# Feed-forward weight slices in four buffers, loaded in one schedule across the phases

## What is computed

```python
def _reference_tuple_inner(x, W_r, W_k, W_v, mu_r, mu_k):
    x_prev = jnp.concatenate([jnp.zeros((B, 1, C), x.dtype), x[:, :-1, :]], axis=1)
    xr = mu_r * x + (1.0 - mu_r) * x_prev
    xk = mu_k * x + (1.0 - mu_k) * x_prev
    r = jax.nn.sigmoid(jnp.einsum('btc,dc->btd', xr, W_r))
    k = jnp.einsum('btc,dc->btd', xk, W_k)
    k_act = jnp.square(jax.nn.relu(k))
    out = r * jnp.einsum('btc,dc->btd', k_act, W_v)
...
xn = _layernorm(x, axis=-1)
x = x + _L0_attn_ref(xn, Wq, bq, Wk, bk, Wv, bv) + _L0_ffn_ref(xn, W_r, W_k, W_v, mu_r, mu_k)
```

## Time and profile before

| | us |
|---|---|
| median of 2 runs | 5767.32 (5766.93 to 5767.71) |
| the profiled execution | 5756.6 |
| its span (slowest core, core 0) | 5755.0 |
| spans of the 8 cores | 5732.4 to 5755.0 |
| granted TensorE clock, mean of a core | 0.761 to 0.768 |
| feed-forward stage, first slice load to the last store | 866 to 2152 |
| stage of the attention | from about 2260 |

### The profile page before, as it was taken

How to read it: one execution, slowest core, us unless ns; L and a number is a source line. 1 busy time by engine, 2 the same in 40 slices (tenths; PEclk the granted TensorE clock), 3 DMA queues, 4 the chain that set the end, 5 groups by cost and what they waited for, 6 DMA issues and landing times.

```text
span 5755.0 us, 57304 instructions; the slowest of 8 cores (5732.4 to 5755.0 us)
## 1 busy us (share of the span) xinstructions
PE 3132.9 (54%) x11513; PEld 1102.6 (19%) x11513; DVE 2488.8 (43%) x5263; ACT 1707.0 (30%) x2627; POOL 286.9 (5%) x301
## 2 busy tenths in 40 slices
PE   1121203332433432777777777777777678678676
PEld 0021101111111111122222222122122123122122
DVE  3431313444343331652753753643643653653653
ACT  2300000000000000255355355355255245245255
POOL 0000010000000000000000000000000000000000
PEclk9965557677767776688788688688688689689688
DMA  1244002111211121110110110110110100100100
GB/s 61 61 78 92 5 3 52 40 40 38 51 40 48 46 57 26 28 28 11 27 28 11 27 28 12 27 28 10 28 28 5 34 19 14 34 19 14 28 19 17
DMA packets 516779, 181.70 MB, mean 32 GB/s; under 512 B 494282, under 2 KB 495474, under 8 KB 516274
## 3 DMA queue, kind: packets, MB, share of 16 engines
q1 hardware_dynamic: 482386, 130.46, 10.0%
q0 software_dynamic: 34080, 47.56, 4.5%
HBM read 142.23 MB, written 39.34 MB: 32 GB/s over the span
## 4 chain that ended last, share of the span: by engine, by line
PE 35%; DVE 21%; DMA 17%; ACT 13%; issue 10%; DVEq 1%; ACTq 1%; POOL 0%; SPq 0%; POOLq 0%
PE pS L847 9%; DVE bm L773 8%; ACT aT L862 7%; PE pO L815 7%; PE pA L762 7%; PE pA L1008 4%; PE pA L516 3%; DMA fW<-wT_r 3%; DMA fW<-wT_k 3%; PE pA L1069 2%; ACT stage L943 2%; DMA fW<-wT_v 2%; DMA nb<-norm_all 2%; DVE fA L501 2%; DVE bis_ge L409 1%
## 5 line engine op out<-in xcount | busy, mean ns | idle before, releaser
L773 DVE TENSOR_REDUCE bm<-pA 128x16 f32<-128x512 f32 x1664 | 1151.1, 692 | 605.1 <-PE pA L762 470.3
L862 ACT ACTIVATE aT<-pS 128x1024 bf16<-128x1024 f32 x1024 | 1047.7, 1023 | 772.4 <-PE pS L847 731.1
L815 PE MATMUL pO<-aT,vtm 128*65 128x512 bf16 x2048 | 698.2, 426 | 311.7 <-ACT aT L862 310.9
L762 PE MATMUL pA<-ktp,qtp 64*128 64x512 bf16 x1664 | 685.0, 422 | 312.2 <-ACT aT L862 110.3
L847 PE MATMUL pS<-rhsc,lhsc 128*128 128x512 bf16 x2048 | 714.5, 438 | 0.0
L516 PE MATMUL pA<-fA,fW 128*128 128x512 bf16 x1536 | 416.4, 424 | 282.6 <-DMA fW<-wT_r 77.4
L417 PE MATMUL pB<-bis_cnt,ones 128*128 128x32 f32 x116 | 35.2, 397 | 682.4 <-DVE bis_cnt L413 682.4
L815 PEld LDWEIGHTS pO<-aT,vtm 128*65 128x65 bf16 x2048 | 234.3, 122 | 648.5 <-issue 501.5
L773 DVE TENSOR_REDUCE bm<-pO 128x16 f32<-128x512 f32 x384 | 265.6, 692 | 212.4 <-PE pO L762 177.7
L762 PEld LDWEIGHTS pA<-ktp,qtp 64*128 64x128 bf16 x1664 | 152.4, 95 | 881.6 <-issue 878.2
L516 PEld LDWEIGHTS pA<-fA,fW 128*128 128x128 bf16 x1536 | 152.1, 106 | 541.5 <-issue 431.9
(11 more groups left out here) (150 smaller groups left out, 2542.9 us busy)
## 6 DMA issues: line engine op xcount, KB each, us to landing
xtile<-x SPq DMA_DIRECT2D x64, 512.0 KB
fW<-wT_r SPq DMA_DIRECT2D x64, 256.0 KB
fW<-wT_k SPq DMA_DIRECT2D x64, 256.0 KB
fW<-wT_v SPq DMA_DIRECT2D x64, 256.0 KB
out<-stage SPq DMA_DIRECT2D x32, 512.0 KB
rhsc<-qtp POOLq DMA_DIRECT2D x32, 256.0 KB, 3.6
lhsc<-ktp POOLq DMA_DIRECT2D x32, 256.0 KB, 2.8
bx<-bsm_dram POOLq DMA_DIRECT2D x32, 256.0 KB, 8.1
```

The source lines that it names most:

```text
L762: e.matmul(pap, qtp[p0:p0 + 64, ts0 + t * 128:ts0 + (t + 1) * 128], ktp[p0:p0 + 64, ts0 + kq * 512:ts0 + (kq + 1) * 512], start=True, stop ...
L773: e.tensor_reduce(bmp[:, kq * 16:(kq + 1) * 16], pap.rearrange("p (k e) -> p k e", e=32), axis=AX.X, op=ALU.max))
L815: e.matmul(pO[0:65, sl * 512:(sl + 1) * 512], vtm[:, (sq * 16 + k) * 130 + hip * 65: (sq * 16 + k) * 130 + hip * 65 + 65], aT[bpar][:, sl ...
L862: e.activation(aT[bpar][:, :], pS[bpar][:, :], AF.Exp, scale=0.125))
```

## The change

There are four buffers `fW` in place of two, and the 192 slice loads (8 quarters, 3 weights, 8 slices) form one list. Loads 0 to 3 are issued ahead of the loop. After the matmuls of slice i, wherever in the three phases it stands, the load of slice i + 4 is issued; it waits for the matmuls of slice i, whose buffer it takes. The last four slices of a phase so issue the first four loads of the next phase, the ones of v2 those of the next quarter. SP's wait for TensorE's counter at each phase's head is gone. The number of loads, their size, their queue and the recorder's wait between them are the same. The diff:

```diff
@@ -474,8 +474,8 @@
             fB = st_p0.enter_context(nc.sbuf_tensor("fB", [128, 8 * QT], BF))
             fR = st_p0.enter_context(nc.sbuf_tensor("fR", [128, 8 * QT], BF))
             fF = st_p0.enter_context(nc.sbuf_tensor("fF", [128, 8 * QT], BF))
-            fW = [st_p0.enter_context(nc.sbuf_tensor("fW0", [128, 8 * 128], BF)),
-                  st_p0.enter_context(nc.sbuf_tensor("fW1", [128, 8 * 128], BF))]
+            fW = [st_p0.enter_context(nc.sbuf_tensor(f"fW{j}", [128, 8 * 128], BF))
+                  for j in range(4)]
             ptile = st_p0.enter_context(nc.sbuf_tensor("ptile", [128, C], BF))
             ptileb = st_p0.enter_context(nc.sbuf_tensor("ptileb", [128, C], BF))
             ptile2 = [ptile, ptileb]
@@ -519,6 +519,21 @@
                                     start=(cc == 0), stop=(cc == 7)))
                 return r.cnt["sPE"]
 
+            wsched = [(tag, d) for _Q in range(8)
+                      for tag in ("r", "k2", "v2") for d in range(8)]
+            wst = {"ld": {}, "mm": {}}
+
+            def wload(i):
+                if i >= len(wsched):
+                    return
+                if i - 4 >= 0:
+                    r.wait("sync", "sPE", wst["mm"][i - 4])
+                tag, d = wsched[i]
+                wst["ld"][i] = load_wslice(fW[i % 4], tag, d)
+
+            for i in range(4):
+                wload(i)
+
             for Q in range(8):
                 t0 = Q * QT
                 mu_mix(fA, "r", t0)
@@ -529,20 +544,16 @@
                         emit_bisect_iter(it)
                 cons = [r.cnt["sAC"], r.cnt["sAC"]]
                 r.wait("tensor", "sDV", r.cnt["sDV"])
-                npe_hist = [0] * 8
-                r.wait("sync", "sPE", r.cnt["sPE"])
-                lds = [load_wslice(fW[0], "r", 0), load_wslice(fW[1], "r", 1)]
                 for d in range(8):
                     par = d % 2
-                    r.wait("tensor", "sSY", lds[d])
+                    gi = Q * 24 + d
+                    r.wait("tensor", "sSY", wst["ld"][gi])
                     if d == 0:
                         r.wait("tensor", "sDV", ndv_mixr)
                     r.wait("tensor", "sAC", cons[par])
-                    npe_q = mm_quarter("r", fA, d, fW[par], par)
-                    npe_hist[d] = npe_q
-                    if d + 2 < 8:
-                        r.wait("sync", "sPE", npe_hist[d])
-                        lds.append(load_wslice(fW[par], "r", d + 2))
+                    npe_q = mm_quarter("r", fA, d, fW[gi % 4], par)
+                    wst["mm"][gi] = npe_q
+                    wload(gi + 4)
                     r.wait("scalar", "sPE", npe_q)
                     cons[par] = r.emit("scalar", lambda e, d=d, par=par: e.activation(
                         fR[:, d * QT:(d + 1) * QT], pA[:, par * 512:par * 512 + QT],
@@ -556,20 +567,16 @@
                         emit_bisect_iter(it)
                 consd = [r.cnt["sDV"], r.cnt["sDV"]]
                 r.wait("tensor", "sAC", r.cnt["sAC"])
-                npe_hist = [0] * 8
-                r.wait("sync", "sPE", r.cnt["sPE"])
-                lds = [load_wslice(fW[0], "k2", 0), load_wslice(fW[1], "k2", 1)]
                 for d in range(8):
                     par = d % 2
-                    r.wait("tensor", "sSY", lds[d])
+                    gi = Q * 24 + 8 + d
+                    r.wait("tensor", "sSY", wst["ld"][gi])
                     if d == 0:
                         r.wait("tensor", "sDV", ndv_mixk)
                     r.wait("tensor", "sDV", consd[par])
-                    npe_q = mm_quarter("k2", fA, d, fW[par], par)
-                    npe_hist[d] = npe_q
-                    if d + 2 < 8:
-                        r.wait("sync", "sPE", npe_hist[d])
-                        lds.append(load_wslice(fW[par], "k2", d + 2))
+                    npe_q = mm_quarter("k2", fA, d, fW[gi % 4], par)
+                    wst["mm"][gi] = npe_q
+                    wload(gi + 4)
                     r.wait("vector", "sPE", npe_q)
                     consd[par] = r.emit("vector", lambda e, d=d, par=par: e.tensor_scalar(
                         fB[:, d * QT:(d + 1) * QT], pA[:, par * 512:par * 512 + QT],
@@ -584,18 +591,14 @@
                 r.wait("tensor", "sAC", nac_sq)
                 consd = [r.cnt["sDV"], r.cnt["sDV"]]
                 r.wait("tensor", "sAC", r.cnt["sAC"])
-                npe_hist = [0] * 8
-                r.wait("sync", "sPE", r.cnt["sPE"])
-                lds = [load_wslice(fW[0], "v2", 0), load_wslice(fW[1], "v2", 1)]
                 for d in range(8):
                     par = d % 2
-                    r.wait("tensor", "sSY", lds[d])
+                    gi = Q * 24 + 16 + d
+                    r.wait("tensor", "sSY", wst["ld"][gi])
                     r.wait("tensor", "sDV", consd[par])
-                    npe_q = mm_quarter("v2", fA, d, fW[par], par)
-                    npe_hist[d] = npe_q
-                    if d + 2 < 8:
-                        r.wait("sync", "sPE", npe_hist[d])
-                        lds.append(load_wslice(fW[par], "v2", d + 2))
+                    npe_q = mm_quarter("v2", fA, d, fW[gi % 4], par)
+                    wst["mm"][gi] = npe_q
+                    wload(gi + 4)
                     r.wait("vector", "sPE", npe_q)
                     consd[par] = r.emit("vector", lambda e, d=d, par=par: e.tensor_tensor(
                         fF[:, d * QT:(d + 1) * QT], pA[:, par * 512:par * 512 + QT],
```

## The result

The changed kernel takes 5609.6 us (median of 10 runs, 5602.9 to 5683.1) against 5766.9 (median of 8). In the run of 5683.1 us the cores of one die had a granted clock of 0.74 against 0.76 on the others, and it is left out of the ratio. The ratio, of the means of the runs, is 0.9738, with a 95% interval of 0.972 to 0.9755: 2.6% faster, about 151 us (the two medians lie 157 us apart).

The account below looks back on a forecast made before the run. Serial slice loads on SP, not TensorE, were taken to bound the feed-forward phases. Terms of 149 + 12 - 2 - 8 = 151 us took the median of 5767.3 us to a forecast of 5616 us, range 5598 to 5650.

Parts of the forecast that it names:

- What bounds a phase: In the feed-forward phases SP's loads run strictly one after the other and set the rate, about 3.04 us each.
- Part 1: Inside the 24 feed-forward phases, two of six load steps of 3.1 us fall away: 149 us gained.
- TensorE would not become the bound: In a phase, loads let slice 7 start at 16.1 us, TensorE at worst 16.0; rival chance 0.06.
- four or five slices without a gap and three behind gaps: On TensorE's trace of a phase: the first four or five slices run gapless, three gaps for loads remain.
- Part 2: At the heads of 15 r and k2 phases, the first slice starts 0.8 us sooner: 12 us gained.
- starts about 0.15 us after that: At r and k2 heads, the first slice follows the end of DVE's last bisection instruction by about 0.15 us.
- Part 3: From k2 to v2, the four early loads land with 0.5 us to spare; 2 us lost, between 0 and 11.
- Part 4: At quarter ends, the next quarter's early loads meet the stores to part_sc: 8 us lost, between 0 and 24.
- The sign of being wrong: At quarter ends, stores to part_sc taking over 3.5 us each would show the forecast wrong.
- Sum: Over the whole run, 149 + 12 - 2 - 8 = 151 us gained, to 5616 us, 2.6% less.
- The slower one: Rival: TensorE's clock stays at 1.2 GHz through whole phases, 80 us slower, 5847 us; chance 0.03.
- The one with faster loads: Rival: loads get faster and TensorE alone paces phases of about 16.2 us, gain 196 us, 5571 us; chance 0.03.

Follow-up runs that it names:

- e3: The changed kernel with eight buffers fW in place of four: 5578.8 us, 0.9691 of the kernel before.
- e4: The changed kernel, four buffers kept, with loads counted by two semaphores in turn so that two are in flight: 5556.7 us, 0.9644 of the kernel before.
- run 67: No label, but words of "made the run 67 us faster": the changed kernel with waits already covered in the same queue left out, 5542.5 us, 0.9621 of before.

## Why the prediction was right, and where its terms were off

The time was 5609.6 against 5616 predicted. By its steps:

- **What bounds a phase.** Right. The load chain is serial before and after, and the number of its steps inside a phase, not the number of buffers as such, makes the time. The kernels with two, three, four and eight buffers have phases of 23.89, 20.91, 17.84 and 16.26 us.
- **Part 1, two steps a phase, 149 us.** 579.5 less 428.1 us is 151.4, but sets core 0 beside core 7; on either core alone it is 152.9. A phase was forecast at 18.0 us and takes 17.84. That TensorE would not become the bound held, with 1.6 to 1.7 us of room (the phases of e3 and e4). The detail of four or five slices without a gap and three behind gaps was off: six run through and two wait, because the loads, which run on at 3.0 us, are ahead of the matmuls until the sixth slice. The waits put down to loads sum to 36.5 us for the same reason, not to 50 to 70.
- **Part 2, heads, 12 us.** The mechanism was right, the size wrong: 5 us on core 0, and 6.8 on core 7. The mean head of the 15 phases went from 3.37 to 45.5 / 15 = 3.03 us. The step that failed is "starts about 0.15 us after that", taken from the nearest rows without counting what else stands in TensorE's queue: four more waits, fulfilled, at 0.1 us each. The same cost was already in the trace of before, in the 0.46 us between ACT's last square and v2's first matmul.
- **Part 3, v2's loads in time.** Right, and the 2 us put aside for it were not needed. v2 heads stay at 7.2 to 7.6 us as before, and v2 phases are no longer than the others.
- **Part 4, the collision, 8 us, bound 24.** It exists and costs 2.5 to 3 us. The Trainium skill (DMA: Bandwidth & Descriptors, Issuing engines are not separate DMA queues) gives the sign, and the experiment with the loads behind the barrier agrees with it, 71.36 to 68.78 us. The bound took a whole load's engine time for each of three stores; the first two stores lost 0.5 us each in quarter 1, the third nothing. The sign of being wrong, a store of over 3.5 us, could not tell: on cores 0 and 7 the longest store takes 4.1 to 4.7 us before and 4.4 to 4.5 with the change.
- **Sum.** On core 0 the terms make 152.9 + 5.0 - 2.5 = 155.4 us where the stage lost 155.2, on core 7 152.9 + 6.8 - 3.0 = 156.7 where it lost 155.9. That the forecast of 151 us came so close owes something to luck: 5 to 7 us too many for the heads stand against 4 too few for the phases, 5 too many for the collision and 2 for late loads.
- **Rivals.** The slower one, a clock that stays low, did not come near: in the phase of the chain above the first slice takes 3.59 us and the last 1.90. The one with faster loads did not happen in the change, but its end is what e4 shows when the loads may overlap: 16.11 us a phase where the rival had 16.2.

By the cost model of the Trainium skill (DMA: Bandwidth & Descriptors, its two cost components), a fit to DMAs issued from GpSimd, a step was estimated at 2.7 us. These loads are issued from SP, and the steps measured by taking buffers away are 2.98 and 3.07 us, so the row stays the better guide. In the same model 2.0 of a load's 2.6 us don't depend on its bytes. That fits e4, where loads of 2.9 to 3.5 us each are issued 1.73 us apart.

## What to carry to other kernels

Where loads on one queue wait for each other, buffers only move load steps out of the stretch in which they are exposed: count steps between the first and last consumer, times the serial load time, until the consumer bounds. Letting two loads fly, with a semaphore for each parity, needs no further memory. With four buffers it brought more than four more buffers did (53 us against 31), with two buffers less than a third one (49 against 67). Before taking a start as "releaser plus one wait's latency", count the waits in that engine's queue, and drop those that an earlier wait of the same queue covers.

## What was not expected of the hardware

- A wait that is already fulfilled costs TensorE's queue 0.10 to 0.12 us when it stands behind the wait that blocks, and nothing when it stands ahead of it (10.86 us with and without ten more). Leaving out 7309 of 22970 entries of TensorE's queue, and 230 of the other queues, made the run 67 us faster.
- Two slice loads in flight took the pace from 3.0 us a slice to at most 2.0, the matmuls' own. A load still lands 2.9 to 3.5 us after its issue, but the next is issued after 1.73 us.
